# The first transfers of a fused decoder layer: another order, another split over the three issuing engines, and a semaphore of its own for gamma and beta

## The reference, cut to what matters

```python
x = layernorm(x + attn(x))        # linear attention with rotary embedding, 16 heads
x = layernorm(x + cross(x, ctx))  # softmax attention over 77 context tokens, 16 heads
x = layernorm(x + ffn(x))         # 16 experts, top 4 by the router, 128 -> 256 -> 128

# in attn
q = gelu(x @ Wq.T + bq) + 0.21
k = gelu(x @ Wk.T + bk) + 0.21
v = x @ Wv.T + bv
...                               # rope, kv = k^T v per head, out = q kv z
res = out + x
return (res - mean) / sqrt(var + 1e-12) * gamma + beta
# in cross
Q, K, V = x @ Wq + bq, ctx @ Wk + bk, ctx @ Wv + bv
return softmax(Q K^T / sqrt(8)) V @ Wo + bo
```

## Time and profile before

| | |
|---|---|
| median of three runs | 633.91 us (633.74 to 634.24) |
| the profiled execution | 632.64 us, span 630.6 us |
| mean granted TensorE clock | 0.981 |
| TensorE (PE) busy | 591.0 us |
| VectorE, ScalarE, GpSimd busy | 418.8, 406.4, 242.8 us |

### The profile page before, as it was taken

The page is one execution under the profiler, slowest core; times in us unless marked ns, Lnnn a source line. Parts: engine busy times, 40 slices in busy tenths (PEclk is TensorE's granted clock), DMA queues, the critical chain, the costliest instruction groups (busy, mean ns, idle before and its releaser), DMA issues. The chain is left out here.

```text
span 630.6 us, 16584 instructions
## 1 busy us (share of the span) xinstructions
PE 591.0 (94%) x6513; PEld 431.7 (68%) x6513; DVE 418.8 (66%) x1472; ACT 406.4 (64%) x519; POOL 242.8 (38%) x166
## 2 busy tenths in 40 slices
PE   5897988999999999999999999999999999899995
PEld 2543654777668867777677867886778766676664
DVE  2356576666786788677877678678867775365445
ACT  2307727796559856786569665985579657965651
POOL 5235333343253435253444325343425342134242
PEclk9888998999999999999999999999999999999999
DMA  6632020010200120011100120012000110000000
GB/s 145 183 86 76 32 60 28 20 29 1 70 20 3 46 61 28 4 45 29 51 12 2 55 60 19 4 45 65 25 3 19 29 43 5 19 1 2 1 18 18
DMA packets 31541, 23.05 MB, mean 37 GB/s; under 512 B 2744, under 2 KB 30152, under 8 KB 31464
## 3 DMA queue, kind: packets, MB, share of 16 engines
q1 hardware_dynamic: 24120, 16.75, 9.2%
q10 hardware_dynamic: 6992, 4.81, 2.7%
q0 software_dynamic: 352, 0.43, 0.4%
HBM read 13.90 MB, written 5.46 MB: 31 GB/s over the span
## 5 line engine op out<-in xcount | busy, mean ns | idle before, releaser
L713 ACT ACTIVATE g<-ps,b 128x512 f32<-128x512 f32 x256 | 168.2, 686 | 86.2 <-PE ps L1000 85.0
L533 POOL TENSOR_TENSOR gl<-g,gh 128x1024 f16<-128x1024 f32 x64 | 138.3, 2161 | 212.4 <-ACT gh L702 212.4
L1358 DVE SCALAR_TENSOR_TENSOR acc<-ps,cw,acc 128x128 f32<-128x128 f32 x448 | 125.4, 342 | 103.0 <-PE ps L1023 57.3
L1023 PEld LDWEIGHTS ps<-w,g 128*128 128x128 f32 x1024 | 121.6, 192 | 9.8 <-issue 4.6
L1023 PE MATMUL ps<-w,g 128*128 128x128 f32 x1024 | 127.0, 277 | 0.1
L998 PE MATMUL ps<-x2h,w1h 128*128 128x512 f16 x256 | 98.2, 384 | 8.8 <-ACT g L713 8.1
L999 PE MATMUL ps<-x2l,w1h 128*128 128x512 f16 x256 | 97.6, 381 | 0.0
L1000 PE MATMUL ps<-x2h,w1l 128*128 128x512 f16 x256 | 97.5, 381 | 0.0
L1019 PE MATMUL ps<-w2h,gh 128*128 128x128 f16 x512 | 89.2, 219 | 1.7 <-DVE acc L1358 1.5
L1021 PE MATMUL ps<-w2h,gl 128*128 128x128 f16 x512 | 89.0, 219 | 0.0
L1020 PE MATMUL ps<-w2l,gh 128*128 128x128 f16 x512 | 89.0, 219 | 0.0
(11 more groups left out here) (188 smaller groups left out, 864.6 us busy)
## 6 DMA issues: line engine op xcount, KB each, us to landing
q_rep<-q_parts SPq DMA_DIRECT2D x24, 128.0 KB
x<-in_x SPq DMA_DIRECT2D x8, 256.0 KB, 3.3
w_stage<-in_L_ffn_w ACTq DMA_DIRECT2D x1, 2048.0 KB, 13.2
q_swap<-q SPq DMA_DIRECT2D x16, 128.0 KB, 2.4
q_parts<-qx SPq DMA_DIRECT2D x16, 128.0 KB, 1.7
k_rep<-k_parts SPq DMA_DIRECT2D x24, 77.0 KB
out<-fin SPq DMA_DIRECT2D x7, 256.0 KB, 2.5
cx<-in_ctx SPq DMA_DIRECT2D x8, 154.0 KB
```

Of the source, the lines that this page charges most:

```text
L533: pool.tensor_tensor(gl[:, j % SPLIT_RING, :, :], g32[:, e % RING, :, :], gh[:, j % SPLIT_RING, :, :], ALU.subtract).then_inc(s["lo"], 1)
L713: act.activation(g32[:, e % RING, h, :], bH[:, h, :], ACT.Gelu, bias=b1[:, e, h:h + 1], scale=1.0 / WS).then_inc(s["gelu"], 1)
L1023: m = pe.matmul(o, g32[:, e % RING, h, tok], w2[:, j, h, :], start=(h == 0), stop=(h == HALF - 1))
L1358: m = dve.scalar_tensor_tensor(out=(acc_all if e == E - 1 else acc)[:, b, :], in0=second_bank(f, e)[:, b * P:(b + 1) * P], scalar=cw[:, b, ...
```

## The change

Three lists of transfers are changed. On SP the rows bk and bv go right behind `x`, the three bias columns behind them, and gamma and beta last. The context of group 0 leaves SP and goes on ACT's queue, behind the constants and ahead of `b1_in`. On POOL the weights Wk and Wv go first, then the row bv, then Wq, Wo, the row bo and rb. Gamma and beta are counted on a new semaphore `ld_gb`; the waits follow: `kv01` on VectorE waits for two transfers on `ld_wide` instead of four, `x_beta` on POOL waits for `ld_gb` instead of `ld_wide`, and `norm1` on VectorE has a new wait for `ld_gb`. Every transfer of before is still there, with the same shape; none is added.

```diff
@@ SP
             load_x(0)
+            for i, n in enumerate(("L0_attn_bk", "L0_attn_bv")):
+                sp.dma_start(wide[:, i, :], row(n).broadcast_to([P, P])).then_inc(s["ld_wide"], 16)
             for to, n in ((bq, "L0_attn_bq"), (xbq, "L0_xattn_bq"), (xbk, "L0_xattn_bk")):
                 sp.dma_start(to[:, :], A[n].rearrange("(n a) -> n a", a=1)).then_inc(s["ld_b"], 16)
-            for i, n in enumerate(("L0_attn_bk", "L0_attn_bv", "L0_attn_gamma", "L0_attn_beta")):
-                sp.dma_start(wide[:, i, :], row(n).broadcast_to([P, P])).then_inc(s["ld_wide"], 16)
-            load_cx(0)
+            for i, n in enumerate(("L0_attn_gamma", "L0_attn_beta")):
+                sp.dma_start(wide[:, 2 + i, :], row(n).broadcast_to([P, P])).then_inc(s["ld_gb"], 16)
             swap(0)
@@ POOL
-            for i, n in enumerate(("L0_xattn_bv", "L0_xattn_bo")):
-                pool.dma_start(wide[:, 4 + i, :], row(n).broadcast_to([P, P])).then_inc(s["ld_xwide"], 16)
+            for i, n in ((1, "L0_xattn_Wk"), (2, "L0_xattn_Wv")):
+                pool.dma_start(xw[:, i, :], A[n]).then_inc(s["ld_xw"], 16)
+            pool.dma_start(wide[:, 4, :], row("L0_xattn_bv").broadcast_to([P, P])).then_inc(s["ld_xwide"], 16)
+            for i, n in ((0, "L0_xattn_Wq"), (3, "L0_xattn_Wo")):
+                pool.dma_start(xw[:, i, :], A[n]).then_inc(s["ld_xw"], 16)
+            pool.dma_start(wide[:, 5, :], row("L0_xattn_bo").broadcast_to([P, P])).then_inc(s["ld_xwide"], 16)
             pool.dma_start(rb[:, :], row("L0_ffn_router_b").broadcast_to([P, E])).then_inc(s["ld_xwide"], 16)
-            for i, n in enumerate(("L0_xattn_Wq", "L0_xattn_Wk", "L0_xattn_Wv", "L0_xattn_Wo")):
-                pool.dma_start(xw[:, i, :], A[n]).then_inc(s["ld_xw"], 16)
@@ POOL, x_beta
-                    pool.wait_ge(s["ld_wide"], 16 * 4)
+                    pool.wait_ge(s["ld_gb"], 16 * 2)
@@ ACT
             act.dma_start(cst[:, P:], consts[:, P:]).then_inc(s["ld_c"], 16)
+            act.dma_start(cx[:, :, :], cx_dram[0]).then_inc(s["ld_cx"], 16)
             act.dma_start(b1_in[:, :], A["L0_ffn_b1"].rearrange("e (h n) -> (e h) n", h=HALF)).then_inc(s["ld_b1"], 16)
@@ VectorE, kv01 and norm1
-                            dve.wait_ge(s["ld_wide"], 16 * 4)
+                            dve.wait_ge(s["ld_wide"], 16 * 2)
...
                     since(dve, "res", a + 1)
+                    dve.wait_ge(s["ld_gb"], 16 * 2)
                     moments(0, res, a, "y1", "st1", "ag1", "ve1", 1e-12)
```

More of the change, by code:

```diff
@@ L270, in build @@
         bH = ps[:, 6:8, :]
-        names = """ld_id ld_c ld_b1 ld_wide ld_xwide ld_xw ld_b ld_in ld_w1 ld_w2 ld_w2s ld_x ld_cx ld_swap ld_rep ld_mx st_k st_qh st_ql st_out
+        names = """ld_id ld_c ld_b1 ld_wide ld_gb ld_xwide ld_xw ld_b ld_in ld_w1 ld_w2 ld_w2s ld_x ld_cx ld_swap ld_rep ld_mx st_k st_qh st_ql st_out
             i_ones i_idle i_idb i_rows i_wt i_wtc i_wtl i_b1t i_b2 i_b2h i_b2l i_wh i_ws i_wl i_w2 i_rw i_rwl i_v1 i_lg
```

## The result

The changed kernel took 628.29 us (median of four runs, 626.19 to 629.56), against 633.85 before: the ratio, worked out over paired runs, is 0.9907 with a 95% interval of 0.9883 to 0.9932. That is 5.6 to 5.9 us, where 3.4 was forecast. The median, 628.29, lies just inside the lower end of the forecast range, 628.2, and the time by the ratio, 0.9907 times 633.85 = 627.96, lies outside it. The profiled execution of the changed kernel is its slowest of the four: 629.56 us, span 627.1, mean clock 0.975.

The account below looks back on a forecast made before the run. TensorE's matmuls bound the steady state from 110 to 600 us, so only its start could move. v1 3.4 us sooner, other parts 0: 633.9 − 3.4 = 630.5 us from the median, range 628.2 to 633.1.

Parts of the forecast that it names:

- Both gates: First pass, ahead of v1: TensorE's 4.02 us wait for the context, then ACT's copy of it, held by rw until 17.62.
- With its landing kept: ACT's wait for rw: rw lands as before, the context's copy ends at 18.33, v1 starts about 18.4, 3.4 us sooner.
- the two zeros for SP's and POOL's orders: First-pass transfer lists: bk and bv early on SP worth 0; POOL's order costs nothing, its bv copy hidden by 2.2 us.
- The context's landing: Start-up: issued on ACT's queue, the context lands at 14.1 instead of 16.6; bounds 13.1 and 16.6.
- The rule that spreading over queues doesn't help: Context on ACT's queue: by the rule the sum would be zero; the prediction said bytes are reordered, as w_stage falls behind.
- ld_b: Bias columns behind bk and bv on SP: wanted by q at 12.62, landed by 10.9, 1.7 us to spare, cost 0.
- I take the clock as kept: TensorE's 12 fillers ahead of kv01: idle stretch shrinks from 4.0 to 1.5 us, full clock stays, fillers take 2.8 us.
- Rival B: First pass: rw lands 2 us sooner, v1 at 17.2 to 18.1; fillers ahead of x1_t give up to 1.57; 628.4; 16%.
- I find no other time that is fixed to the clock on the wall: Behind the first pass: later transfers are issued by program steps and move along, so the 3.4 us carries through.
- Rival A: Start-up: the context lands no sooner, at 15.3 or later; at 15.9 with half clock a gain of 0.7, 633.2; 12%.
- C: Start-up: ACT is held at its seventh issue, b1, until the context lands; kv01 at 22.7, 1.6 us slower, 635.5; 6%.
- The costs put at nothing: First pass: new waits for gamma and beta, POOL's bv copy ending about 17.2, four weights landed by 16.6: no cost.

Follow-up runs that it names:

- ctx_alone: The kernel before with only the context of group 0 moved to ACT's queue behind the constants, other transfers in the old order; ratio 0.9931.
- again: The changed kernel run once more with no edit; ratio 0.9917 to the kernel before.
- gb_late: The kernel before with gamma and beta issued behind the swap of q on their own semaphore, context still on SP; ratio 0.9936.
- cols_late: The kernel before with the three bias columns behind the four broadcast rows on SP, context still last; ratio 0.999.
- pool_alone: The kernel before with only POOL's order changed as in the change; ratio 1.0033.
- before_fill: The kernel before with eight more filler matmuls in the second pass, four ahead of each of den and out; ratio 0.9973.

## Why the prediction was wrong

The direction was right and the size was too small. Both gates that I read showed: the context in the changed kernel's first wait, `rw` in ctx_alone and again. In the first profile of the changed kernel slow fillers, and not `rw`, decided v1. Point by point:

- **The step that failed** is "With its landing kept", with the sentence before it, "the bytes before it are the same", and the two zeros for SP's and POOL's orders. I took the order within a queue to move only that queue's own landings. The changed kernel had the constants 2.8, `rw` 1.4 and the first weights 1.2 us sooner, with the same bytes ahead of each. v1 then stood 4.4 us sooner, in both profiles, and not 3.4. ctx_alone, where the orders are kept, had v1 at 18.37 against my 18.4; the term was right for the edit it described.
- **The rest of the excess**, 1.2 to 1.5 us, is in neither profile: their spans are 627.1 and 627.4, 3.5 and 3.2 us under 630.6. Over all runs (the point on the profiled execution, below) the means are only 4.5 us apart, so this rest may be scatter; the record doesn't settle it.
- **The context's landing** (14.1, bounds 13.1 and 16.6) was mis-sized. ctx_alone has 13.15, the lower bound, which was made by bytes. The changed kernel has 12.15 in one profile and had it by 11.09 in the other, both below the bound. The rate up to 12.6 us was 149 and 150 GB/s there, and not the 124 that I carried over.
- **The rule that spreading over queues doesn't help** (the Trainium skill, "DMA: Bandwidth & Descriptors", "Rules for kernel authors") was read in the prediction as no gain. It speaks of bandwidth, and it leaves the issue time that is saved. In ctx_alone the context was issued 3.83 us sooner and stood 3.45 us sooner, and gb_late, with the context issued at 3.69 on its old queue, has nearly the same ratio (0.9936 beside 0.9931). So no run contradicts the rule: what counted was what stood ahead of the bytes that someone waited for, and no run shows that the other queue was needed. Whether the move itself raises bandwidth stays open; ctx_alone's profile has 132 and 282 GB/s up to 12.6 and from there to 16.6 us, where that of before has 124 and 250.
- **`ld_b`**: no transfer is wanted at 12.62 but at the table load ahead of q. Before, that ran at 10.87; in the changed kernel it waited 0.89 us for the columns, and 3.62 in cols_late. My 1.7 us of cover were none. It cost nothing in the changed kernel, as ACT waited 3.71 us for `rw` behind q anyway.
- **The clock**: "I take the clock as kept" failed in the profiled execution (4.27 us for the fillers) and held in again (then the gate decides). By either way v1 came at 17.4, which is chance. Rival B's other half, up to 1.57 us at the fillers ahead of x1, came in the first profile, with 1.19 at the fillers and 0.47 at the matmuls ahead of them. In again the low clock behind the wait for the copy cost 1.33 us there instead.
- **"I find no other time that is fixed to the clock on the wall"** missed that the granted clock can take time back: 2.6 us behind x1 in the profiled execution. Thus its span, 627.1, agrees with the forecast 627.2 by luck: 1.0 at v1 and 1.66 ahead of x1 cancel with the 2.6.
- **The profiled execution as a measure.** That of before had a clock at the top of its kind, that of the changed one near the bottom. Over all runs, 77 of before and 10 of the changed kernel (changed and again), the means are 633.20 us at 0.9751 and 628.69 at 0.9814, 4.5 us apart. A straight line through the 77 has 0.30 us less for a clock 0.001 higher (correlation -0.53), so some 1.9 of the 4.5 go with the clock. This is an estimate, and which causes which was not tried beyond the fillers.
- Rival A (the context no sooner) and C (ACT held) didn't come: the context's issue took 0.64 us. The costs put at nothing for gamma and beta, for POOL's copy (14.57) and for the four weights hold.

What stays open: how one queue's order moves the landings of another. The runs show for POOL's order that it does. For SP's the single profiles point the same way: with POOL's old order, `rw` landed at 13.2 to 14.4 in six profiles with SP's new order and at 15.5 to 17.6 in three with the old. They don't show the mechanism.

## What to carry to other kernels

Where an engine waits for a first transfer, ask what stands ahead of its bytes in its own queue. Don't take the landings of the other queues as fixed: change one list at a time, and read all landings again. Behind a removed wait the next one was readable in the old trace (`rw`, hidden by 3.4 us), and one number in a table moved it out of the way. A position gained early can be lost later, so read one further down as well, here the first expert matmul. In a start-up with fillers, one profile is one draw of the clock; a gain of under 1% needs the clock of each run beside its time.

## What was unexpected of the hardware

- 8 KB of broadcast `rb` took 5.4 us from issue to landing as POOL's third transfer, 9.8 us as its seventh in the changed kernel and 11.7 in pool_alone; it was issued 2.1 us later in these. Over all profiles it took 5.2 to 8.3 us as the third and 9.4 to 11.7 as the seventh.
- The kernel before and before_fill are the same up to the second pass, yet `rw` landed near 17.6 in one and 15.5 in the other, and the context at 16.60 and 15.89. The chip and the execution aren't told apart in this. Landings of single profiles are good to 1 or 2 us, so in the table only differences that several kernels share should be trusted.
- Four runs of the kernel before lay within 0.5 us (633.74 to 634.24); 77 later ones reached from 628.91 to 636.74.
